# Input products of a state space stage, made and signalled per channel group

## The reference

```python
dt, Bm, Cm = jnp.split(x_dbl, [DT_RANK, DT_RANK + D_STATE], axis=-1)
dt = jax.nn.softplus(dt @ dt_proj_w.T + dt_proj_b)
deltaA = jnp.exp(dt[..., None] * A)
deltaBu = (dt * xc)[..., None] * Bm[:, :, None, :]
def step(hst, inp):
    dA, dBu, Ct = inp
    hst = dA * hst + dBu
    y = jnp.einsum('bdn,bn->bd', hst, Ct)
    return (hst, y)
```

## Time and profile before

| | |
|---|---|
| median of 3 runs | 3214.25 us (3213.52 to 3217.51) |
| the profiled execution | 3196.49 us, its span in the trace 3194.7 us |
| state space stage, first product to last scan | 1577.8 to 2635.4 us of the span |
| busy over the span | PE 2642.7, DVE 1914.6, POOL 1375.3, ACT 1097.8 us |
| VectorE's products L1714 | 256, 314.5 us busy |
| VectorE's scans L1721 | 512, 620.0 us busy |

### The profile page before, as it was taken

One profiled execution on the slowest core, in us unless ns is written; L12 is line 12 of the kernel. 1 busy time (PEld: TensorE's weight loads), 2 busy tenths in 40 slices (PEclk: granted clock), 3 DMA queues, 4 the chain that ended last, 5 costly groups with the idle time before them and its releaser, 6 DMA issues. The chain is left out here.

```text
span 3194.7 us, 36195 instructions
## 1 busy us (share of the span) xinstructions
PE 2642.7 (83%) x12202; PEld 1809.3 (57%) x12202; DVE 1914.6 (60%) x3369; ACT 1097.8 (34%) x1765; POOL 1375.3 (43%) x862
## 2 busy tenths in 40 slices
PE   6773499854999999997588897888878677997998
PEld 3331366644999999997233343333433334666997
DVE  6999678463212122222989999998999995331211
ACT  6775122100111111111555645546455431221111
POOL 0000234345333333332168778687786850112332
PEclk9886699955999999998699998999989888998999
DMA  3000100012899999986300010000100001116996
GB/s 114 0 0 0 45 13 20 13 41 98 318 324 325 324 325 327 319 308 223 106 33 34 27 34 33 33 34 27 36 31 33 34 27 34 40 40 239 349 347 238
DMA packets 95181, 395.13 MB, mean 124 GB/s; under 512 B 21366, under 2 KB 48518, under 8 KB 72544
## 3 DMA queue, kind: packets, MB, share of 16 engines
q1 hardware_dynamic: 73472, 351.46, 31.4%
q0 software_dynamic: 21600, 42.37, 3.6%
HBM read 364.94 MB, written 39.29 MB: 127 GB/s over the span
## 5 line engine op out<-in xcount | busy, mean ns | idle before, releaser
L1331 POOL TENSOR_TENSOR ss_h<-ss_h,ss_cs 128x2048 f32<-128x2048 f32 x127 | 574.4, 4525 | 75.1 <-DVE ss_h L1721 67.1
L1418 PE MATMUL ss_y<-ss_h,all_ident 128*128 128x512 f32 x1016 | 520.3, 661 | 49.3 <-POOL ss_h L1331 49.3
L1176 DVE TENSOR_TENSOR experts_in<-experts_sil,experts_pU 128x512 f32<-128x512 f32 x176 | 121.3, 689 | 635.4 <-PE experts_pU L1120 635.4
L1721 DVE TENSOR_TENSOR_SCAN ss_h<-ss_da,ss_c_h,ss_dbu 128x512 f32<-128x512 f32 x384 | 470.8, 1268 | 7.1 <-ACT ss_da L1575 0.3
L1418 PEld LDWEIGHTS ss_y<-ss_h,all_ident 128*128 128x128 f32 x1016 | 213.3, 214 | 323.0 <-issue 260.9
L1575 ACT ACTIVATE ss_da<-ss_dt,ss_decay 128x512 f32<-128x512 f32 x512 | 326.7, 711 | 103.7 <-DVE ss_h L1721 65.2
L1714 DVE TENSOR_TENSOR ss_dbu<-ss_dtx,ss_bB 128x1024 f32<-128x1024 f32 x256 | 314.5, 1229 | 62.2 <-PE ss_bB L1408 36.3
L1120 PE MATMUL experts_pG<-experts_xt,experts_wa 128*128 128x128 f32 x2816 | 346.5, 277 | 0.9 <-DMA experts_wa<-in_w_all 0.9
L1120 PE MATMUL experts_pU<-experts_xt,experts_wa 128*128 128x128 f32 x2816 | 344.1, 275 | 0.0
L1129 PE MATMUL experts_pY<-experts_wa,experts_in 128*128 128x256 f32 x1408 | 332.7, 379 | 0.0
L1120 PEld LDWEIGHTS experts_pG<-experts_xt,experts_wa 128*128 128x128 f32 x2816 | 331.6, 193 | 1.7 <-ACT experts_xt L1146 1.1
(11 more groups left out here) (327 smaller groups left out, 3681.6 us busy)
## 6 DMA issues: line engine op xcount, KB each, us to landing
experts_wa<-in_w_all SPq DMA_DIRECT2D x176, 1536.0 KB, 9.1
ss_cs<-ss_c_rows SPq DMA_DIRECT2D x64, 512.0 KB, 3.6
moe_rows<-route_xn SPq DMA_DIRECT2D x16, 512.0 KB, 3.7
ss_h<-moe_ys SPq DMA_DIRECT2D x5, 1024.0 KB, 7.7
all_x<-in_x SPq DMA_DIRECT2D x8, 512.0 KB, 9.1
gf_xb<-in_x SPq DMA_DIRECT2D x8, 512.0 KB, 3.8
moe_rows<-all_x SPq DMA_DIRECT2D x8, 512.0 KB, 3.6
experts_xr<-moe_rows,moe_token POOLq DMA_INDIRECT x176, 8.0
```

The lines of the kernel that those rows point to most:

```text
L1176: nc.vector.tensor_tensor(IN[t.two][:].rearrange("p f t -> p (f t)"), SIL[t.two][:], pU[t.two][:], ALU.mult)\
L1331: pool.tensor_tensor(h[:], h[:], CS[q % 2][:, n % GROUP].unsqueeze(1).to_broadcast([P, CI, BT]), ALU.mult)\
L1418: mm = pe.matmul(y[:, c], ident[:], H[(b * N + n) % RING][:, c], start=(n == 0), stop=(n == N - 1))
L1721: ins = V.tensor_tensor_scan(H[(b * N + n) % RING][:, c], DA[(b * N + n) % AHEAD][:, c], DBU[:, c % 2], first, ALU.mult, ALU.add)
```

## The change

The product over two groups (128 x 1024) becomes two products of one group (128 x 512), each with its own `dbu_done`. Each scan raises `scanned` of its own. The order on VectorE is: product c, product c+1, scan c, scan c+1. Product c waits for the scan before the last one (`scanned` up to step * 4 + c - 1), and scan c waits for the product of its own group, one instruction further back than before. The two semaphores now count four a step, and all who wait on them count so: GpSimd, TensorE and ScalarE wait for the same events as before. Nothing else is changed; the number of scans, matmuls, activations and transfers is the same, and VectorE has 256 instructions more.

```diff
 def half_step(b, n, half):
-    k = (b * N + n) * 2 + half
+    step = b * N + n
+    pair = (2 * half, 2 * half + 1)
     wait(dve, "dtx_done", b * 2 + half + 1)
-    wait(dve, "spread", b * N + n + 1)
-    wait(dve, "scanned", k)
-    part = slice(2 * half, 2 * half + 2)
-    V.tensor_tensor(DBU[:], DTX[b % 2][:, part], bB[:].unsqueeze(1).to_broadcast([P, 2, BT]), ALU.mult)\
-        .then_inc(s["dbu_done"], 1)
-    wait(dve, "dbu_done", k + 1)
-    wait(dve, "da_done", b * N + n + 1)
-    wait(dve, "summed", b * N + n + 1 - RING)
-    for c in (2 * half, 2 * half + 1):
+    wait(dve, "spread", step + 1)
+    for c in pair:
+        wait(dve, "scanned", step * CI + c - 1)
+        V.tensor_tensor(DBU[:, c % 2], DTX[b % 2][:, c], bB[:], ALU.mult).then_inc(s["dbu_done"], 1)
+    wait(dve, "da_done", step + 1)
+    wait(dve, "summed", step + 1 - RING)
+    for c in pair:
+        wait(dve, "dbu_done", step * CI + c + 1)
         first = 0.0 if starts_at(b) else c_h[:, n, c:c + 1]
-        ins = V.tensor_tensor_scan(H[(b * N + n) % RING][:, c], DA[(b * N + n) % AHEAD][:, c], DBU[:, c % 2], first, ALU.mult, ALU.add)
-    ins.then_inc(s["scanned"], 1)
+        V.tensor_tensor_scan(H[step % RING][:, c], DA[step % AHEAD][:, c], DBU[:, c % 2], first, ALU.mult, ALU.add)\
+            .then_inc(s["scanned"], 1)
```

More of the change, by code:

```diff
@@ L1322, in _ @@
                             gate(b - 1)
-                        wait(pool, "scanned", (b * N + n + 1) * 2 - (1 if not prep and n == N - 1 else 0))
+                        wait(pool, "scanned", (b * N + n + 1) * CI - (2 if not prep and n == N - 1 else 0))
                         h = H[(b * N + n) % RING]
@@ L1338, in _ @@
                 pool.tensor_tensor(last[:, 0:2], last[:, 0:2], row, ALU.mult).then_inc(s["last_product"], 1)
-                wait(pool, "scanned", NB * N * 2)
+                wait(pool, "scanned", NB * N * CI)
                 pool.tensor_tensor(last[:, 2:4], last[:, 2:4], row, ALU.mult).then_inc(s["last_product"], 1)
@@ L1406, in spread @@
                     wait(pe, "bc_done", b + 1)
-                    wait(pe, "dbu_done", (b * N + n) * 2)
+                    wait(pe, "dbu_done", (b * N + n) * CI)
                     pe.matmul(bB[:], SEL[:, n:n + 1].to_broadcast([P, P]), BC[b % 2][:], start=True, stop=True)\
@@ L1487, in _ @@
                 wait(pe, "z_done", NB * CI)
-                wait(pe, "dbu_done", NB * N * 2)
-                wait(pe, "scanned", NB * N * 2)
+                wait(pe, "dbu_done", NB * N * CI)
+                wait(pe, "scanned", NB * N * CI)
                 for c in range(CI):
@@ L1570, in decays @@
                     k = b * N + n
-                    wait(act, "scanned", (k - AHEAD + 1) * 2)
+                    wait(act, "scanned", (k - AHEAD + 1) * CI)
                     if k < AHEAD:
```

## The result

| | before | after |
|---|---|---|
| median of 4 runs each | 3215.69 us | 3193.13 us (3192.73 to 3195.95) |
| ratio | | 0.9932, 95% interval 0.9920 to 0.9944 |
| stage, first product to last scan, in the profiled execution | 1057.6 us | 1035.2 us |
| VectorE's product and scans, a half, without stalls | 3.85 us | 3.54 us |

What follows compares the result with a forecast made beforehand. GpSimd's chain was taken to bound step 10 to step 1, mostly TensorE's bodies step 1 to step 10, VectorE block 7. Terms -7.2 - 9.7 + 1.5 - 2.3 = -17.7 us took 3214.25 to 3196.5, range 3182 to 3209.

Steps and rivals of the forecast that it cites:

- VectorE's own time: VectorE's product and scans in the state space stage: a half falls from 3.85 to 3.58 us, products 0.61 apart.
- The last part: Block 7 from step 1, 118.5 us, bound by VectorE alone: 7.2 us less.
- The six stretches: Step 1 to step 10, six times: TensorE's bodies take back most of the gain, leaving 1.62 us each, 9.7 less.
- The seven stretches: Step 10 to step 1 of the next block, seven times: GpSimd's chain fixes the length, 1.5 us more in sum.
- Block 0: Block 0 to step 10, 82.3 us: TensorE decides at steps 3 and 6, 2.3 us less.
- (a): Rival for the whole stage: VectorE bounds all, so the whole 61 us arrive, 3153 us; chance 0.03.
- (b): Rival on VectorE: no overlap within one PSUM tile, a half takes 4.05 us, 26 us slower, 3240; chance 0.06.
- (c): Rival: no measurable change, from a dearer split product or from TensorE's clock; chance 0.14 for both forms.

Runs made afterwards that it cites:

- e5: Changed kernel without low_part, three GpSimd instructions (twice a block) that correct the logarithm: 0.9822 of the kernel before.
- e3: Changed kernel with the first low_part instruction, a tensor_scalar, moved from GpSimd to VectorE: 0.9939 of the kernel before.
- e9: Changed kernel with low_part's tensor_scalar moved from GpSimd to ScalarE as two activations: 3151.51 us, 0.9862 of the kernel before.
- e4: Kernel before with low_part's tensor_scalar moved from GpSimd to VectorE: 1.0058 of the kernel before.
- e10: Kernel before with low_part's tensor_scalar moved from GpSimd to ScalarE as two activations: 0.9990 of the kernel before.
- e11: Kernel before with the product's wait for the scans put first of its three waits, without a split: 0.9976 of the kernel before.
- e12: Changed kernel with waits on the instruction just before, these placed first so they sit on the instructions: 1.0004 of the kernel before.
- e1: Changed kernel, same instruction order, but each wait on the instruction just before again: 3234.73 us, 1.0058 of the kernel before.
- e2: Changed kernel in the order product, scan, product, scan, each scan waiting for the product just before: 3272.79 us, 1.0171 of the kernel before.

## Why the prediction was right

Forecast 3196.5 within 3182 to 3209, measured 3193.13. Forecast gain 17.7 us, measured 22.6 in the median and 22.4 in the stage. The mechanism and the places are those forecast. Of the four terms below the misses of the first two cancel, 1.2 us each; the other two make up the 4.7 us by which the gain was larger.

- **VectorE's own time.** 3.58 a half was forecast, 3.54 measured: the products are 0.58 apart, the low bound, and not 0.61. The last part shows it pure: 7.2 forecast, 8.4 measured; 15 x 7.08 + 2.61 + 1.2 is 110.0, and its row has 110.1. One reading behind it was off: of the four L1756 only the first and the last wait for the L1752 two places ahead, and the one in the earlier trace rows for that three places ahead. The first does overlap: it begins at 2640.95, while the L1752 just before it runs to 2641.03.
- **The six stretches.** 9.7 forecast, 8.5 measured (76.6 each for 76.3). Body 1 at 5.03, body 2 at 14.81 and body 7 at 58.02 were forecast for block 3, and are 4.98, 14.69 and 57.90; TensorE's idle time before the first two is 0.76 and 0.75, where I had it near 1. What was small was left out: split_bc now waits 0.40 for ScalarE's rows, and in block 3, one of the two that are 77.0 long, step 10 waits 0.41 for the spread, behind a dt_proj body run partly at the half clock (0.50 from 2063 to 2069).
- **The seven stretches.** +1.5 forecast, -0.3 measured. The reading that GpSimd's chain pins them was right, as e5 shows. Two of the seven were 54.1 and 54.3 long in place of 56; in the rest the add-up behind the chain took 5.40, partly at the half clock (0.50 from 1992 to 1993; the clock granted over the whole is 0.68 in the rows above, and 0.72 over the 5.13 of the earlier trace rows). That the term came out near nothing is in part luck: in the stretch of 54.3, which was 55.7 before, this add-up ran at 3.70, and with 5.40 the sum would have grown.
- **Block 0.** 2.3 forecast, 5.2 measured: the term with the largest miss. I took TensorE's bodies as fixed. Its first convolution in the stage took 5.89 us before, at a granted clock of 0.60 over step 2, and takes 3.70 now, at 0.93. The convolution and the window of that step, in the kernel before and in the changed one:

```profile
1595.16 5.89 PE L1374 MATMUL ss_q<-ss_xr,ss_tap 128*128 128x512 f32 x8 [0.69 <-ACT ss_xr L1522]
...
1592.80:1601.40 8.60, 7.78 (x11) 2.44 (x10) 7.16 (x7) 3.36 (x6) 5.78 (x4) 0.60 0.20 61
```

```profile
1613.55 3.70 PE L1374 MATMUL ss_q<-ss_xr,ss_tap 128*128 128x512 f32 x8 [0.69 <-ACT ss_xr L1522]
...
1611.30:1618.10 6.80, 5.55 (x13) 1.94 (x11) 6.80 (x9) 3.73 (x6) 4.72 (x2) 0.93 0.12 44
```

  That is 2.2 us of the 2.9 missed. It goes with the faster VectorE and isn't chance: block 0 takes 77.0 to 77.3 in after, e3, e5 and e9, and 81.8 to 82.5 in before, e4, e10, e11 and e12, in both groups of runs. Why the clock rises sooner wasn't tried and is open.
- **The rivals.** (a), all 61 us, fell: only with low_part and three taps left out is its order of gain reached (68.3). (b), no overlap, fell: products and scans overlap across the one PSUM tile by 0.09 to 0.12, and the same instructions take 4.02 (e1) or 3.54 us a half by their waits alone. (c), no change that can be measured, had two forms: a half of 3.82, if a split product costs 0.73 and not 0.61, or a gain that TensorE's clock takes back. No run shows those 0.12 in the changed kernel: without a stall its products are 0.58 apart, the first scan begins 0.12 before the second product ends, and the half is 3.54. e12 has a half of 3.82 by another way, with gaps of 0.03 to 0.04 and no overlap between products and scans, and its ratio of 1.0004 bears out what (c) made of it. The clock didn't take the gain back either: the seven stretches are 388.8 and 388.5 us, the six 8.5 us shorter.

My expectations did worse than the prediction where I put a wait that ends last at 0.03 wherever it stood (e1, e2), and where I moved work between engines by duration alone (e3, e4).

## What to carry to other kernels

VectorE's chain of dependent instructions paid 0.03 or 0.13 us here at each link where the wait named the instruction just before. Interleaved as two independent chains, with each wait on the instruction before last, it had overlaps of 0.09 to 0.12 in place of these gaps. The wait that will end last should come first in the program, so that it sits on the instruction: here that took 0.10 off a half (e11). But price such a gain stretch by stretch: here two thirds of it went to the next bounds, and relieving one of them was worth nothing before the change and 22 to 26 us after it.

## What the runs showed of the hardware that I had not expected

- A wait that ended last cost 0.03 to 0.04 us where it sat on the waiting instruction (e11, e12) and 0.13 to 0.14 us where a separate wait instruction ahead of it held it (before, e1, e2); the program's first wait got the place on the instruction (3.85 to 3.75 by moving one line, e11).
- A `tensor_scalar` of 128 x 1024 fp32 on VectorE took 0.69 us alone and up to 3.59 us beside GpSimd's products, where each of 14 ended 0.54 to 0.56 us after the product it had met (e3), while the scans with `c_h`, which ran beside the same products all along, have a mean of 1.268 us before and after.
- The same instructions ahead of the stage took 1578 to 1580 us in some groups of runs and 1597 to 1601 in others. Chip 7 had both; why is open.
